# Selecting routed nodes among 45 finished blocks beside the gathers, the last four by pairwise ranking

## The reference, cut to what matters

```
hx    = einsum('ni,rio->rno', layernorm(x), weight)      # 8 relations
agg   = segment_sum(hx[edge_type, src], dst)
x     = x + agg * 0.5**0.5 + h_bias + layernorm(x) @ loop_weight * 0.5**0.5
xn    = layernorm(x)
w     = xn @ wr + br                                       # one routing weight for each node
sel   = the 3124 nodes with the largest w (top_k of half of them, less the last)
y     = (gelu(xn[sel] @ w1 + b1) @ w2 + b2) * w[sel]
x     = x + xn, and + y at the selected nodes
```

## Time and profile before

| what | value |
|---|---|
| median of 3 runs (lowest to highest) | 2099.67 us (2099.63 to 2100.09) |
| profiled execution: time, span | 2100.03 us, 2098.4 us |
| busy, TensorE matmul / VectorE / ScalarE / POOL | 1717.8 / 793.3 / 734.9 / 1525.2 us |
| mean granted clock of TensorE | 0.948 of full |

### The profile page before, as it was taken

The page is one execution under the profiler, slowest core; times in us unless marked ns, Lnnn a source line. Parts: engine busy times, 40 slices in busy tenths (PEclk is TensorE's granted clock), DMA queues, the critical chain, the costliest instruction groups (busy, mean ns, idle before and its releaser), DMA issues.

```text
span 2098.4 us, 30549 instructions
## 1 busy us (share of the span) xinstructions
PE 1717.8 (82%) x8696; PEld 1459.7 (70%) x8696; DVE 793.3 (38%) x1880; ACT 734.9 (35%) x1524; POOL 1525.2 (73%) x1615
## 2 busy tenths in 40 slices
PE   2796898988888788888888888888888888898883
PEld 1585687767776677777667767767777777777773
DVE  8743343343333334233432333343333334333337
ACT  6733333333332333242333323332422333333242
POOL 7777777777777777777777777777777777777730
PEclk9998899999999999999999999999999999999995
DMA  8953433433433433433433343433333343343336
GB/s 326 325 162 107 127 105 110 124 107 107 126 106 107 125 107 107 126 107 106 125 109 106 116 117 107 117 115 107 117 116 106 116 117 107 112 122 105 105 89 219
DMA packets 126310, 265.88 MB, mean 127 GB/s; under 512 B 32206, under 2 KB 72957, under 8 KB 126138
## 3 DMA queue, kind: packets, MB, share of 16 engines
q0 software_dynamic: 76704, 209.56, 34.3%
q1 hardware_dynamic: 37002, 42.02, 6.1%
q10 hardware_dynamic: 12432, 12.32, 1.8%
HBM read 244.53 MB, written 19.25 MB: 126 GB/s over the span
## 4 chain that ended last, share of the span: by engine, by line
POOL 51%; issue 18%; PE 15%; SPq 6%; DMA 5%; DVE 3%; ACT 2%; DVEq 0%; ACTq 0%; POOLq 0%
POOL messages L487 50%; PE bank L796 5%; PE bank L828 4%; SPq L428 4%; DMA messages<-normed_table,gather_rows 3%; PE bank L859 2%; PE bank L849 2%; SPq L418 1%; DMA closed<-in_x 1%; DVE acc L1303 1%; ACT hidden L655 1%; PE bank L806 1%; DMA normed_table<-closed 1%; PE bank L830 0%; SPq L425 0%
## 5 line engine op out<-in xcount | busy, mean ns | idle before, releaser
L487 POOL DMA_INDIRECT messages<-normed_table,gather_rows x1550 | 1474.0, 951 | 472.2 <-issue 461.5
L796 PE MATMUL bank<-messages,onehot 128*128 128x256 f32 x3196 | 836.2, 398 | 314.2 <-DMA messages<-normed_table,gather_rows 240.9
L796 PEld LDWEIGHTS bank<-messages,onehot 128*128 128x128 f32 x3196 | 581.0, 196 | 424.9 <-DMA messages<-normed_table,gather_rows 282.9
L1137 DVE SCALAR_TENSOR_TENSOR sums<-bank,regular,sums 128x256 f32 x538 | 260.0, 483 | 1215.3 <-PE bank L806 1174.1
L607 ACT ACTIVATE stage<-bank 128x256 f32<-128x256 f32 x538 | 206.6, 384 | 1286.6 <-PE bank L796 1273.0
L828 PE MATMUL bank<-rel_sb,closed 128*128 128x256 f32 x1568 | 356.8, 381 | 0.1
L828 PEld LDWEIGHTS bank<-rel_sb,closed 128*128 128x128 f32 x1568 | 299.2, 191 | 42.2 <-issue 0.8
L1055 DVE TENSOR_TENSOR onehot<-bank,keys 128x768 f32<-128x768 f32 x269 | 254.7, 947 | 1.2 <-issue 1.2
L806 PE MATMUL bank<-ident,stage 128*128 128x128 f32 x1076 | 209.0, 276 | 3.6 <-ACT stage L607 3.2
L859 PE MATMUL bank<-w_sb,hidden 128*128 128x256 f32 x784 | 198.4, 410 | 11.2 <-ACT hidden L655 11.1
L849 PEld LDWEIGHTS bank<-normed_t,w_sb 128*128 128x128 f32 x1568 | 200.7, 207 | 3.1
(11 more groups left out here) (163 smaller groups left out, 587.3 us busy)
## 6 DMA issues: line engine op xcount, KB each, us to landing
side<-normed_table SPq DMA_DIRECT2D x2048, 1.0 KB
messages<-normed_table,gather_rows POOLq DMA_INDIRECT x1550
acc<-in_x SPq DMA_DIRECT2D x12, 512.0 KB, 12.6
residual<-resid ACTq DMA_DIRECT2D x12, 512.0 KB
node_out<-acc SPq DMA_DIRECT2D x12, 512.0 KB
normed_x<-normed_table ACTq DMA_DIRECT2D x11, 512.0 KB, 4.2
messages<-residual SPq DMA_DIRECT2D x6, 896.0 KB, 10.3
rel_sb<-in_L_gnn_weight SPq DMA_DIRECT2D x2, 1024.0 KB, 8.8
```

Of the source, the lines that this page charges most:

```text
L487: pool.indirect_dma_start(messages[0:EP, g % RING, j * D:(j + 1) * D], None, x if g < RAW else table, bass.IndirectOffsetOnAxis(ap=gather_ ...
L796: last = nc.tensor.matmul(banks[g % STAGES][:, 0:D], onehot[0:EP, g % SLOTS, j, :], rows, start=(j == 0), stop=(j == J - 1))
L1137: V.scalar_tensor_tensor(sums[:, :, to], banks[TURNS[g % 2]][:, 0:D].rearrange("p (n m) -> p n m", m=W), regular[:, 0:1], sums[:, :, to], ...
```

## The change

The selection's eight rounds leave the end. They are made in ticks 505 to 521 among the 45 blocks (5760 nodes) whose weights are then known, and for two thresholds at once: 490 nodes are still open, so the 3124th largest of all lies between the (3124 - 490)th and the 3124th largest of the known. All 15 candidates are compared on VectorE (`ask`), for both thresholds; ScalarE's signs are gone. TensorE adds the counts in the tick behind each `ask`, VectorE takes them in the next (`answer`). The 490 known nodes between the two thresholds are then packed into four columns of 128 (ticks 523 to 533: `in_between` with some 10 operations before its signal and 10 after it, `places_of`, twelve one-hot packs in bf16 with 45 matmuls, `unpack` with 18 operations). These four columns and those of blocks 45 to 48 are ranked by pairwise comparison: TensorE turns a column into a row on all partitions (`turn_row`), and `insert(c)` compares it with all columns before it, in ticks 535 to 542 for the first seven and after the loop for the last. The node of rank 490 is the last one kept; its key is handed to all partitions and compared with all keys. `ffn_first` and `ffn_second` of block 48 come after that on TensorE. `ffn_leave` of block 47 moves into the output loop. From tick 505 on `build` reads its numbers from SBUF (`iota0`) instead of a PSUM bank. Scratch lies in the used parts of `gather_rows` and `keys`.

```diff
+    LATE = 4
+    KNOWN = NB - LATE
+    OPEN_NODES = N - KNOWN * P
+    COLUMNS = 2 * LATE
+    DIGITS = 15
+    BYTES = 6
+    PACKED = 4
+    PACKS = -(-KNOWN // PACKED)
     SELECTED = max(1, int(0.5 * N)) - 1
+    TARGETS = (SELECTED - OPEN_NODES, SELECTED)
+    SORT = closes[KNOWN - 1] + LAG + NORM + 1
+    TIES = SORT + 16
+    BETWEEN = SORT + 18
+    PLACES = SORT + 20
+    UNPACK = PLACES + PACKS // 2 + 2
+    INSERT = UNPACK + 2
+    inserts = {INSERT: (0, 1), INSERT + 1: (2,), INSERT + 3: (3,), INSERT + 4: (4,), INSERT + 5: (5,), INSERT + 7: (6,)}
...
+            def total_counts(r):
+                pe.wait_ge(counts_in, r + 1)
+                nc.tensor.matmul(exchange[:, 0:2 * DIGITS], one_rows, pick_counts.rearrange("p t d -> p (t d)"),
+                                 start=True, stop=True).then_inc(counts_out, 1)
...
+            def sum_pack(n):
+                pe.wait_ge(pack_ready, n + 1)
+                for b in range(PACKED * n, min(PACKED * (n + 1), KNOWN)):
+                    last = nc.tensor.matmul(packed_out, packs[n % 2][:, b % PACKED, :], payload[:, b, :, :].rearrange("p h c -> p (h c)"),
+                                            start=(b == 0), stop=(b == KNOWN - 1))
+                last.then_inc(pack_summed, 1)
+            def turn_row(c):
+                if c in (3, 6, 7):
+                    pe.wait_ge(inserted, c)
+                nc.tensor.transpose(turned_rows[c], weights[:, c:c + 1].broadcast_to([P, P]), ident[:, :]).then_inc(row_turned, 1)
+            def select_known(g):
+                if SORT < g < TIES and (g - SORT) % 2 == 1:
+                    total_counts((g - SORT) // 2)
+                if g == TIES + 1:
+                    prefix(8, tied.rearrange("p t b -> p (t b)"), 2 * KNOWN, 2)
+                    nc.tensor.matmul(exchange[:, 0:2], one_rows, above_count, start=True, stop=True).then_inc(counts_out, 1)
+                if g == BETWEEN + 1:
+                    prefix(9, between, KNOWN, 0).then_inc(counts_out, 1)
+                if PLACES < g < UNPACK:
+                    for n in (2 * (g - PLACES) - 2, 2 * (g - PLACES) - 1):
+                        if n < PACKS:
+                            sum_pack(n)
+                if g == INSERT - 1:
+                    pe.wait_ge(weights_ready, 1)
+                    for c in range(3):
+                        turn_row(c)
+                if g == INSERT + 2:
+                    for c in range(3, 6):
+                        turn_row(c)
+                if g == INSERT + 6:
+                    pe.wait_ge(weights_ready, 2)
+                    turn_row(6)
             for g in range(TICKS):
                 if LAG <= g < NG + LAG:
...
-            nc.tensor.matmul(banks[2][:, 0:NB], before[:, :], tied[:, :], start=True, stop=True).then_inc(counts_out, 1)
-            ffn_second(NB - 1, HC // 2, HC)
+                select_known(g)
+            pe.wait_ge(weights_ready, 3)
+            turn_row(COLUMNS - 1)
+            pe.wait_ge(counts_in, 11)
+            nc.tensor.matmul(exchange[:, 2 * P:2 * P + 3], one_rows, last_parts, start=True, stop=True).then_inc(counts_out, 1)
+            ffn_first(NB - 1)
+            ffn_second(NB - 1)
...
+            def ask(r):
+                step = float(1 << (12 - 4 * (r % 4)))
+                link(pick_step, V.scalar_tensor_tensor(candidates, digits.unsqueeze(1).broadcast_to([P, 2, DIGITS]), step,
+                                                       floors.unsqueeze(2).broadcast_to([P, 2, DIGITS]), ALU.mult, ALU.add))
+                for t in range(2):
+                    of = key_hi[:, 0:KNOWN] if r < 4 else lows[:, t, :]
+                    n = t * DIGITS * KNOWN
+                    last = V.tensor_tensor(compared[:, n:n + DIGITS * KNOWN].rearrange("p (d b) -> p d b", d=DIGITS),
+                                           of.unsqueeze(1).broadcast_to([P, DIGITS, KNOWN]),
+                                           candidates[:, t, :].unsqueeze(2).broadcast_to([P, DIGITS, KNOWN]), ALU.is_ge)
+                    last.then_inc(pick_step, 1)
+                count[pick_step.name] += 2
+                dve.wait_ge(pick_step, count[pick_step.name])
+                V.tensor_reduce(pick_counts.rearrange("p t d -> p (t d)"), compared.rearrange("p (d b) -> p d b", b=KNOWN),
+                                AX.X, ALU.add).then_inc(counts_in, 1)
+            def answer(r):
+                step = float(1 << (12 - 4 * (r % 4)))
+                dve.wait_ge(counts_out, r + 1)
+                link(pick_step, V.tensor_tensor(reached.rearrange("p t d -> p (t d)"), exchange[:, 0:2 * DIGITS],
+                                                enough.rearrange("p t d -> p (t d)"), ALU.is_ge))
+                link(pick_step, V.tensor_reduce(passed, reached, AX.X, ALU.add))
+                link(pick_step, V.scalar_tensor_tensor(floors, passed, step, floors, ALU.mult, ALU.add))
+            def low_halves():
+                link(pick_step, V.tensor_scalar(floors, floors, 0.5, None, ALU.add))
+                high, low = key_hi[:, 0:KNOWN], key_lo[:, 0:KNOWN]
+                for t in range(2):
+                    link(pick_step, V.tensor_scalar(tied[:, t, :], high, floors[:, t:t + 1], None, ALU.is_equal))
+                    link(pick_step, V.tensor_scalar(above[:, t, :], high, floors[:, t:t + 1], 65537.0, ALU.is_gt, ALU.mult))
+                    link(pick_step, V.scalar_tensor_tensor(lows[:, t, :], low, 1.0, tied[:, t, :], ALU.add, ALU.mult))
+                link(pick_step, V.tensor_tensor(lows, lows, above, ALU.add))
+                link(pick_step, V.tensor_scalar(lows, lows, -1.0, None, ALU.add))
+                link(pick_step, V.memset(floors, -0.5))
+            def ties():
+                link(pick_step, V.tensor_scalar(floors, floors, 0.5, None, ALU.add))
+                for t in range(2):
+                    link(pick_step, V.tensor_scalar(above[:, t, :], lows[:, t, :], floors[:, t:t + 1], None, ALU.is_gt))
+                    link(pick_step, V.tensor_scalar(tied[:, t, :], lows[:, t, :], floors[:, t:t + 1], None, ALU.is_equal))
+                V.tensor_reduce(above_count, above, AX.X, ALU.add).then_inc(counts_in, 1)
...
+            def places_of():
+                dve.wait_ge(counts_out, 10)
+                link(pick_step, V.tensor_copy(totals[:, 0, :], exchange[:, 0:KNOWN]))
+                link(pick_step, V.tensor_tensor_scan(bases[:, 0, 1:KNOWN + 1], totals[:, 0, :], zeros, 0.0, ALU.add, ALU.add))
...
+                link(pick_step, V.tensor_scalar(place, place, -1.0, None, ALU.add))
+                for h in range(LATE):
+                    link(pick_step, V.tensor_scalar(tile_masks[:, :, h], totals[:, 1, :], float(h), None, ALU.is_equal))
+                link(pick_step, V.tensor_tensor(payload, tile_masks.unsqueeze(3).broadcast_to([P, KNOWN, LATE, BYTES]),
+                                                key_bytes.unsqueeze(2).broadcast_to([P, KNOWN, LATE, BYTES]), ALU.mult))
+            def build_pack(n):
+                b, past = PACKED * n, min(PACKED * (n + 1), KNOWN)
+                if n >= 2:
+                    dve.wait_ge(pack_summed, n - 1)
+                V.tensor_tensor(packs[n % 2][:, 0:past - b, :], iota0[:, :].unsqueeze(1).broadcast_to([P, past - b, P]),
+                                place[:, b:past].unsqueeze(2).broadcast_to([P, past - b, P]), ALU.is_equal).then_inc(pack_ready, 1)
...
+            def insert(c):
+                dve.wait_ge(row_turned, c + 1)
+                row_c = turned_rows[c]
+                if c < COLUMNS - 2:
+                    link(pick_step, V.tensor_copy(kept_rows[c], row_c))
+                if c:
+                    whole = beaten[:, 0:c * P]
+                    link(pick_step, V.tensor_tensor(whole.rearrange("p (c n) -> p c n", c=c), row_c.unsqueeze(1).broadcast_to([P, c, P]),
+                                                    weights[:, 0:c].unsqueeze(2).broadcast_to([P, c, P]), ALU.is_gt))
+                    link(pick_step, V.tensor_reduce(more[:, 0:c], whole.rearrange("p (c n) -> p c n", c=c), AX.X, ALU.add))
+                    link(pick_step, V.tensor_tensor(rank[:, 0:c], rank[:, 0:c], more[:, 0:c], ALU.add))
+                    n = min(c, COLUMNS - 2) * P
+                    link(pick_step, V.tensor_scalar(beaten[:, 0:n], row_area[:, 0:n], weights[:, c:c + 1], None, ALU.is_ge))
+                if c == COLUMNS - 1:
+                    link(pick_step, V.tensor_scalar(beaten[:, (c - 1) * P:c * P], turned_rows[c - 1], weights[:, c:c + 1], None, ALU.is_ge))
+                own = beaten[:, c * P:(c + 1) * P]
+                link(pick_step, V.scalar_tensor_tensor(own, row_c, weights[:, c:c + 1], lower, ALU.is_equal, ALU.mult))
+                link(pick_step, V.scalar_tensor_tensor(own, row_c, weights[:, c:c + 1], own, ALU.is_gt, ALU.add))
+                link(pick_step, V.tensor_reduce(rank[:, c:c + 1], beaten[:, 0:(c + 1) * P], AX.X, ALU.add))
+                dve.sem_inc(inserted, 1)
```

(45 more changed lines are left out.)

215 lines of the change are left out of this document (123 added, 92 removed).

## The result

The changed kernel takes 2110.31 us (median of 4 runs, 2107.54 to 2111.15) where the kernel before, run beside it, takes 2099.88 (4 runs): ratio 1.0048, interval 1.0035 to 1.0060. That is inside the predicted range, 2.3 us above the forecast of 2108.0 and above the 0.2% that a measurement can tell. The profiled execution has a span of 2109.5 us against 2098.4.

A forecast was written before the change was run, and what follows sets the result against it. POOL's gathers, with TensorE behind, bound the loop. The end at 2098.4, less 15.3 us of idle DMA, plus 24.7 of lateness (12.5 + 12.2), less about 1, gave a span of about 2107 and a time of 2108; range 2096 to 2115.

The forecast's parts named there:

- end = 2083.1 + D: End of the kernel: 2098.4 less the 15.3 us the DMA engines idled during selection, plus D.
- D: How much later block 48 reaches its residual store: 24.7 us, a gain only if below 15.3.
- Tail: Selection left after the loop on VectorE: 10.4 us from weight to first output operation, where it took 35.2.
- D, first part: Ticks 505 to 532: TensorE stands for VectorE's questions and packs; 12.5 us late at tick 532, bounds 0 and 20.
- term by sums (14.7): Ticks 505 to 532: 20.1 us standing plus 6 of new TensorE work, less 11.4 of vanished gather waits.
- lay-out by ticks (10.6): Ticks 505 to 532 laid out tick by tick with TensorE always at its higher clock level: 10.6 us late.
- D, second part: VectorE from tick 535 to block 48's entry: the inserts make it 12.2 us later, bounds 9 and 16.
- Build from SBUF, and POOL: Builds reading SBUF instead of PSUM cost nothing, at most 0.05 us on each of 13; gathers lose 2.8, hidden.
- price of 0.06 for a scalar operation: POOL's gathers lose about 0.06 us per VectorE scalar operation, so the 44 moved beside them cost 2.8 us.
- (a): Ticks swallow the selection and only the inserts cost: 12.2 us late, time 2097 to 2100, no change; chance 0.21.
- (b): Faster: VectorE's durations overlap or prove shorter from tick 535 to 543, inserts hide; time 2085 to 2095; chance 0.14.
- (c): New idle pieces leave TensorE at 1.2 GHz while catching up: 5 to 12 us more, 2113 to 2120; chance 0.12.

The follow-up runs named there:

- x1: Changed kernel with the first seven inserts left out (they only count themselves, ranks zero): 2095.81 us, ratio 0.9977 to the kernel before.
- x2: Changed kernel with each of the eight questions comparing 5 of the 45 columns: 2101.09 us, ratio 1.0007 to the kernel before.
- x3: Changed kernel with the residual's first six pieces loaded without waiting for block 48: 2104.36 us, ratio 1.0020 to the kernel before.
- z2: Kernel before with all builds in the loop (265) reading their numbers from SBUF instead of PSUM: 2163.32 us, ratio 1.0296.
- z1: Kernel before with builds reading their numbers from SBUF instead of PSUM from tick 505 on: 2102.43 us, ratio 1.0010.
- z4: Kernel before with one contiguous in-place scalar operation of 735 elements added on VectorE behind each of 265 builds: 2119.31 us, ratio 1.0074.
- z3: Kernel before with one scalar operation of 735 elements, repeating input, added on VectorE behind each of 265 builds: 2098.98 us, ratio 0.9990.
- y4: Changed kernel with questions and packs in other ticks, inserts 0 to 3 at tick 540, 4 to 6 behind block 48's normalization: 2103.32 us, ratio 0.9995.

## Why the prediction held, step by step

**end = 2083.1 + D.** Right, and 2 us too high: it gives 2111.9, 2096.0 and 2099.7 for the measured D of the changed kernel, x1 and x2, whose spans are 2109.5, 2094.0 and 2097.5. The forecast's "about 1" for writes directly behind loads should have been 2 to 2.4 (19.37 for the twelve pieces).

**Tail.** Predicted 10.4 us; 2067.50 to 2077.92 is 10.4. Selection over before the loads, no idle stretch, block 48's FFN covered: as predicted. x3 tested the order of the bounds: loads first, selection some 5 us of span behind.

**D, first part.** Predicted 12.5, measured 14.9. The standing predicted at ticks 514, 520 and 526 (6.6, 2.6, 4.8) was 7.29, 2.52 and 5.17. Tick 516 stood 1.86 in place of 4.2, since TensorE came late to it: it did two sums at 2.77 and 2.55 after the long wait. Tick 506 stood 3.66, a wait that the forecast took as hidden. The standing came to 20.8 in all, for 20.1. The term by sums (14.7) came close, but partly by luck. From the end of group 503's sum to the end of group 532's TensorE takes 118.0 us (1897.21 to 2015.21) where it took 104.2 (1895.84 to 2000.03), 13.8 more: 20.8 for VectorE as forecast, 1.1 for ScalarE, 8.3 of busy time (94.4 against 86.1) in place of 6, and 16.1 of gather waits gone (17.8 to 1.7) in place of 11.4. Two errors of opposite sign nearly cancel. Another 1.4 was there ahead of the stretch, which makes 15.2 at the end of group 532's sum and 14.9 at tick 535's add. The lay-out by ticks (10.6) was too low, and the value taken between them with it; it lacked the slower sums behind the long waits, 3.2 us in the three behind ticks 514 and 516. The granted clock there, 0.53, goes with their lengths; no run changed the clock alone.

**D, second part.** Predicted 12.2, measured 14.7. Inserts 0 to 6 took 24.2 us in place of 23.4. VectorE's waits between tick 535's add and the entry, priced at 1.7 in all, were some 3.2: three times 0.32 behind an insert, 0.77 and 0.54 for TensorE's turns, and 0.88 for the entry itself, which a relation product of 3.62 in place of 5.30 would have spared. TensorE's 5.54 for `ffn_first` cost nothing: it stood 3.66 for VectorE after it. x1 measures the part: 15.9 at the loads, of which 1.7 lay ahead of it.

**Build from SBUF, and POOL.** The one step that was wrong. "Nothing, at most 0.05 on each of 13" looked at the build's own time and not at POOL; z2 gives 0.25 each, z1 0.18 to 0.22. The price of 0.06 for a scalar operation came from a misread row. The 1.09 at 1980.42 starts inside an operation that the kernel before already has, with both inputs in SBUF, from 1980.27 to 1980.70, and ends 0.81 behind it:

```profile
1980.27 0.43 DVE L1177 TENSOR_TENSOR resid<-x,normed 128x256 f32<-128x256 f32 x1
```

That z4 then measured 0.06 to 0.08 is luck: its operation takes 0.55 us, where those that the change moved take 0.2 to 0.4, which the estimate above puts under 0.04. z3's form costs nothing. In the changed kernel the gathers carry 8.2 us in place of the forecast 2.8, 7.7 of it in the last 120. Its trace says where: from 1890 us on 23 gathers take 1.0 us or more, and each ends 0.82 (within 0.02) behind an operation of VectorE with both inputs in SBUF. Nine are at builds (4.1 us over the usual length), eight at the comparisons of the questions (2.4), three at packs (0.6), one at the payload (0.9) and two at operations that were there before (0.4). The 8.2 us stayed hidden, as the forecast had it for its smaller sum, under TensorE's lag of 15. y4, with less lag, shows that they count when they are not hidden.

The rule weighed in the prediction (the Trainium skill, SBUF — State Buffer, "Who interferes with whom") is exclusion for a whole instruction. The traces agree with it: a gather that starts inside z4's operation waits for its end. What was wrong is the size worked out from it, 0.2 to 0.4 for each operation, because most operations catch no gather; by the estimate above, 0.07. The same section says that an operation with two inputs in SBUF contends with a GpSimd instruction that reads SBUF, and one with a single input outside the two-port modes does not; z2 (0.25 each) and z3 (none) agree, and this was the rule to have weighed.

**Rivals.** (a), only inserts cost, falls: x2 shows the questions worth some 9 us. (b), faster, falls with D = 28.8, far from 11. (c), the clock: present, in the 3.2 us of part one's sums named above and the 0.9 at the entry, and in other sums too (2.77 at 1908.41); the time stays 3 us under that rival's 2113. Its share of D was not measured by itself; the granted clock over the span was 0.944 against 0.948.

**What stays open.** How the 4 us of D that neither x1 nor x2 removes divide, and how y4 would do with its comparisons and builds reading from PSUM, for which this kernel has no free bank.

## What to carry to other kernels

Work that leaves a tail must be charged to the in-order queues that it enters: 35 us of selection left the end, only 15 of them were on the path, and 29 came back as lateness of the last block, because each small question and its sum stand in line with the loop's own work. Before moving work "into idle time", look at the length of the idle pieces, not at their sum, and find the second bound behind the first (here loads, then selection, then POOL). Beside a stream of indirect gathers, count the inputs in SBUF of VectorE's operations, and keep long ones from having two.

## What was not expected of the hardware

A POOL gather that starts while VectorE runs an elementwise operation with both inputs in SBUF, or a contiguous scalar operation (z4), stands still until that operation ends and then needs 0.82 us. On average that is 0.25 us for a build of 0.95 and 0.06 to 0.08 for a scalar operation of 0.55; the longest gather beside the moved work took 1.86 in place of 0.95. With one of the inputs in PSUM, or one repeating input (z3, 0.91 us long), gathers stay at 0.95.
